# A narrow cross attention with its PSUM banks dealt anew and one small operation moved from VectorE to GpSimd

## The reference

```python
def _L0_xattn_ref(hidden_states, encoder_hidden_states, attention_mask, Wq, bq, Wk, bk, Wv, bv, Wo, bo):
    q = (hidden_states @ Wq.T + bq).reshape(B, N, H, D).transpose(0, 2, 1, 3)
    k = (encoder_hidden_states @ Wk.T + bk).reshape(B, T, H, D).transpose(0, 2, 1, 3)
    v = (encoder_hidden_states @ Wv.T + bv).reshape(B, T, H, D).transpose(0, 2, 1, 3)
    scores = jnp.einsum('bhnd,bhtd->bhnt', q, k) * scale + attention_mask[:, None, :, :]
    attn = jax.nn.softmax(scores, axis=-1)
    out = jnp.einsum('bhnt,bhtd->bhnd', attn, v)
    return out.transpose(0, 2, 1, 3).reshape(B, N, C) @ Wo.T + bo

x = x + _L0_xattn_ref(_layernorm(x, axis=-1), ctx_1024, mask_BxSxS2_ff0, ...)
```

## Time and profile before

| | |
|---|---|
| median of three executions | 2395.47 us |
| the profiled execution | 2399.14 us, span 2397.3 us |
| TensorE busy in the span | 2110.9 us (88%) |
| VectorE busy | 1924.7 us (80%) |
| ScalarE busy | 1668.8 us (70%) |
| GpSimd busy | 1200.5 us (50%) |
| narrow cross attention, first load's issue to last residual | 542.7 to 905.2 us |

### The profile page before, as it was taken

The page is one execution under the profiler, slowest core; times in us unless marked ns, Lnnn a source line. Parts: engine busy times, 40 slices in busy tenths (PEclk is TensorE's granted clock), DMA queues, the critical chain, the costliest instruction groups (busy, mean ns, idle before and its releaser), DMA issues. The chain is left out here.

```text
span 2397.3 us, 89507 instructions
## 1 busy us (share of the span) xinstructions
PE 2110.9 (88%) x32271; PEld 1771.4 (74%) x32271; DVE 1924.7 (80%) x5225; ACT 1668.8 (70%) x4485; POOL 1200.5 (50%) x1151
## 2 busy tenths in 40 slices
PE   7999999997777771537999979999799999999997
PEld 7888888885555550235888858888688888888886
DVE  3888888877999986996777667776498999999995
ACT  1676666666777775646888858888476776777674
POOL 0333333326777764107999869999132333333332
PEclk9999999998999995857999989999899999999998
DMA  5000000001111100001000000000133333333333
GB/s 125 3 0 0 0 0 0 0 1 32 31 30 30 30 25 1 1 0 37 1 0 0 0 2 1 0 0 0 52 110 105 115 117 111 115 109 118 113 112 91
DMA packets 112239, 96.98 MB, mean 40 GB/s; under 512 B 24259, under 2 KB 103430, under 8 KB 112134
## 3 DMA queue, kind: packets, MB, share of 16 engines
q1 hardware_dynamic: 108722, 94.39, 12.8%
q10 hardware_dynamic: 3412, 1.19, 0.2%
HBM read 53.59 MB, written 41.94 MB: 40 GB/s over the span
## 5 line engine op out<-in xcount | busy, mean ns | idle before, releaser
L706 POOL TENSOR_TENSOR sa_sc<-sa_sc,sa_rs 128x1024 f32<-128x1024 f32 x64 | 121.8, 1904 | 311.1 <-DVE sa_rs L682 311.1
L1870 POOL TENSOR_TENSOR lo_qk_r<-lo_qk_ms,w_neg_half 128x20 f32<-128x20 f32 x64 | 226.9, 3546 | 22.3 <-DVE lo_qk_ms L1792 22.3
L1870 POOL TENSOR_TENSOR gl_qk_r<-gl_qk_ms,w_neg_half 128x20 f32<-128x20 f32 x64 | 226.3, 3536 | 14.3 <-DVE gl_qk_ms L1792 14.0
L486 POOL TENSOR_TENSOR xan_ve<-xan_mv,w_eps_ln 128x1 f32<-128x1 f32 x64 | 12.1, 189 | 352.8 <-DVE xan_mv L480 352.8
L917 ACT ACTIVATE xa_vx<-xa_oo 64x512 f32<-64x512 f32 x256 | 151.3, 591 | 43.1 <-PE xa_oo L817 38.3
L1015 POOL TENSOR_TENSOR xa_sc<-xa_sc,xa_rs 128x1024 f32<-128x1024 f32 x64 | 122.2, 1909 | 107.3 <-DVE xa_rs L975 107.3
L930 ACT ACTIVATE xa_oT<-xa_oo 128x512 f32<-128x512 f32 x128 | 69.5, 595 | 131.4 <-PE xa_oo L864 131.4
L651 ACT ACTIVATE sa_oT<-sa_oo 128x512 f32<-128x512 f32 x128 | 69.5, 595 | 117.6 <-PE sa_oo L594 117.6
L827 PEld LDWEIGHTS xa_qs<-xan_xT,late_x_wq 128*128 128x128 f32 x1024 | 124.4, 192 | 30.6 <-issue 30.6
L909 ACT ACTIVATE xa_qT<-xa_qs,late_x_bq 128x128 f32<-128x128 f32 x512 | 138.9, 383 | 1.6
L558 PE MATMUL sa_qs<-san_xT,w_a_wq 128*128 128x128 f32 x1024 | 134.0, 285 | 5.4 <-DVE sa_sc L668 5.0
(11 more groups left out here) (323 smaller groups left out, 6714.0 us busy)
## 6 DMA issues: line engine op xcount, KB each, us to landing
blocks<-xa_tb SPq DMA_DIRECT2D x64, 512.0 KB, 2.7
xa_pt<-blocks SPq DMA_DIRECT2D x256, 128.0 KB, 2.9
w_x<-in_x_dram SPq DMA_DIRECT2D x8, 512.0 KB, 7.5
ca_cx<-in_ctx_dram SPq DMA_DIRECT2D x64, 64.0 KB, 1.8
ctxT_kept<-ca_xcT SPq DMA_DIRECT2D x64, 64.0 KB, 1.6
xa_cT<-ctxT_kept SPq DMA_DIRECT2D x64, 64.0 KB, 1.8
out_dram<-xa_out SPq DMA_DIRECT2D x64, 64.0 KB, 1.6
ca_mask<-in_mask_BxSxS_ff_dram SPq DMA_DIRECT2D x64, 32.0 KB, 1.7
```

The costliest lines, as they stand in the source:

```text
L706: pool.tensor_tensor(v, v, bcast(rs[:, s, :], 2, S), ALU.mult).then_inc(prob_done, 1)
L1870: pool.tensor_tensor(qk_r[:, s, :], qk_ms[:, s, :], k["neg_half"][:, 0:NQK], ALU.pow).then_inc(sg["qk_r"], 1)
```

## The change

Numerator and denominator get a bank of their own (`nd`), and the two waits quoted above go. In exchange the transposed probabilities have one bank (`pp`) in place of two: `turn_probs` and `probsT` become two pieces each of half the work, and the second four transposes wait for the copy of the first four. The offset of the norm goes from VectorE (one instruction) to GpSimd (two products of one column: minus the mean, and that times the power), together with a column of -1 set at the start. All lists but GpSimd's get another order, `output` goes from lag 7 to 6 and `residual` from 8 to 7. The sync queue's list is not edited.

```diff
-        off = sb("off", [P, 2])
+        off, neg_mean, neg_one = sb("off", [P, 2]), sb("neg_mean", [P, 2]), sb("neg_one", [P, 1])
         m1, m2 = ps("m1"), ps("m2")
-        pp = [ps("pp0"), ps("pp1")]
+        pp, nd = ps("pp"), ps("nd")
         ss = ctx.enter_context(nc.psum_tensor("ca_ss", [P, 4, 512], F32))
-        num, den = ss[:, 0, 256:384], ss[:, 0, 384:512]
+        num, den = nd[:, 0:P], nd[:, P:2 * P]
...
-                    after(pe, x_done, t, 7)
+                    after(pe, x_done, t, 6)
...
-                    after(pe, o_done, t, 4)
...
-                    pe.wait_ge(biased, min(t + 4, NT) * 2 if isinstance(t, int) else (t + 4) * 2)
...
-                def turn_probs(t, four):
-                    after(pe, exp_done, t)
-                    for b in range(2):
-                        after(pe, p_done, t, 1, per=2)
+                def turn_probs(b):
+                    def piece(t, four):
+                        after(pe, exp_done, t)
+                        if b == 0:
+                            after(pe, p_done, t, 1, per=2)
+                        else:
+                            pe.wait_ge(p_done, t * 2 + 1)
                         for n in range(4):
                             h = 8 * b + 2 * n
-                            last = pe.transpose(pp[b][:, n * P:(n + 1) * P],
-                                                sc[:, four, h:h + 2, :].rearrange("p a b -> p (a b)"), ident)
+                            last = pe.transpose(pp[:, n * P:(n + 1) * P], sc[:, four, h:h + 2, :].rearrange("p a b -> p (a b)"), ident)
                         last.then_inc(p_psum, 1)
+                    return piece
...
-                    pe.wait_ge(xT_done, min(t + 7, NT) if isinstance(t, int) else t + 7)
+                    pe.wait_ge(xT_done, min(t + 6, NT) if isinstance(t, int) else t + 6)
...
-                skewed(pe, NT, [(3, scores), (2, project), (1, turn), (6, attend), (5, turn_probs), (7, output)], 4)
+                skewed(pe, NT, [(6, attend), (3, scores), (5, turn_probs(0)), (2, project), (1, turn), (5, turn_probs(1)), (6, output)], 4)
...
-                skewed(act, NT, [(2, queries_keys), (1, turned), (2, values), (4, exponent), (5, probsT), (0, apply)], 4)
+                skewed(act, NT, [(5, probsT(0)), (2, queries_keys), (1, turned), (5, probsT(1)), (2, values), (4, exponent), (0, apply)], 4)
...
-                skewed(dve, NT, [(8, residual), (0, measure), (3, softmax), (6, normalise), (0, offset)], 4)
+                skewed(dve, NT, [(7, residual), (0, measure), (6, normalise), (3, softmax)], 4)
...
                 def rsqrt(t, four):
-                    norm_rsqrt(k, norm, pool, t, four % 2)
+                    s = four % 2
+                    after(pool, norm["mv_done"], t)
+                    pool.tensor_tensor(neg_mean[:, s:s + 1], norm["mv"][:, s, 0:1], neg_one[:, :], ALU.mult).then_inc(nm_done, 1)
+                    norm_rsqrt(k, norm, pool, t, s)
+                    after(pool, norm["rstd_done"], t)
+                    pool.tensor_tensor(off[:, s:s + 1], neg_mean[:, s:s + 1], norm["rstd"][:, s:s + 1], ALU.mult).then_inc(off_done, 1)
...
+                pool.memset(neg_one[:, :], -1.0).then_inc(minus, 1)
+                pool.wait_ge(minus, 1)
```

More of the change, by code:

```diff
@@ L1061, in narrow_cross_attention @@
                                                               sem("outT_psum"), sem("inverse"), sem("outT"))
-        y_psum, xb_done, x_done, off_done = sem("y_psum"), sem("x_plus_bias"), sem("x"), sem("offset")
+        y_psum, xb_done, x_done, off_done, nm_done, minus = sem("y_psum"), sem("x_plus_bias"), sem("x"), sem("offset"), sem("neg_mean"), sem("minus_one")
         with nc.Block() as block:
@@ L1183, in exponent, with probsT, piece @@
                     act.activation(sc[:, four, :, :], sc[:, four, :, :], ACT.Exp).then_inc(exp_done, 1)
[L1185 to L1188, removed]
+                def probsT(b):
+                    def piece(t, four):
+                        s = four % 2
+                        after(act, a_psum, t, 2)
                         act.wait_ge(p_psum, t * 2 + b + 1)
-                        act.activation(pt[:, s, 4 * b:4 * b + 4, :].rearrange("p a b -> p (a b)"), pp[b][:, :], ACT.Copy).then_inc(p_done, 1)
+                        act.activation(pt[:, s, 4 * b:4 * b + 4, :].rearrange("p a b -> p (a b)"), pp[:, :], ACT.Copy).then_inc(p_done, 1)
+                    return piece
                 def apply(t, four):
@@ L1206, in measure @@
                     norm_measure(k, norm, dve, tile_of(X, t), t, four % 2)
[L1208 to L1213, removed]
                 def softmax(t, four):
```

## The result

The median of four executions is **2356.71 us** (2352.11 to 2357.93); the kernel before, on the same chip, took 2395.30. The ratio is 0.9836, with a 95% interval of 0.9817 to 0.9856: 38.6 us or 1.6% faster. The forecast of 2363.5 was 6.8 us too slow; the time lies in its range, and close to what rival (1) gave.

What follows compares the result with a forecast made beforehand. A VectorE-GpSimd ring through shift and offset sets 5.43 us a step; the new longest ring is 4.89. 57 x (5.43 - 4.89) = 30.8, plus 1: 31.8 off 2399.1, less 3.7 to the runs' median: 2363.5 us, range 2352 to 2385.

Steps and rivals of the forecast that it cites:

- rival (1): ScalarE-TensorE handovers at their low ends, so VectorE's 4.78 us sets the step; 2357 us, chance 0.18.
- Offset to GpSimd: Moving the norm's offset takes one VectorE instruction a step, cuts the old ring, and adds two GpSimd products of 0.15 us.
- the ring above: Old step's ring across GpSimd and VectorE: shift, offset, residual, measure, bias, maximum, shift; 5.43 us a step.
- Own bank: Numerator and denominator's bank: scores and attend lose two waits at no instruction cost, letting attend go first and division precede bias.
- One bank for the transposes: ScalarE and TensorE alternate transposes and copies, exponent to exponent: 4.41 us plus four handovers of 0.12, a ring of 4.89.
- VectorE's floor: VectorE's remaining work per step: 1.20 us for reciprocal and product, 3.58 from residual to maximum, together 4.78.
- GpSimd: GpSimd's own step with the two new products at 0.15 us each: a floor of 4.56 us.
- sign against: VectorE's residual waiting for GpSimd's copy by more than 0.2 us would show the forecast wrong.
- rivals (3) and (4): ScalarE-TensorE handovers of 0.25 make the ring 5.41, about 2394 us, chance 0.05; of 0.34, 5.77, 2414 us, chance 0.09.
- Rival (2): Sync queue's context load lands late, at 3.0 us, making the step 5.24 us; 2383.5 us, chance 0.13.
- The sum: Narrow cross attention: 57 x (5.43 - 4.89) = 30.8 us, plus 1 at the end: 31.8 us saved.
- The end: From last shift to stage end, 11.3 us: 1 us saved by output and residual coming sooner, between nothing and 3.

Runs made afterwards that it cites:

- e1: Kernel before with only the norm's offset moved from VectorE to GpSimd; 2392.77 us, ratio 0.9971.
- e2: Kernel before with the offset left on VectorE, but reading one tensor and the power as a column of scalars; 2390.25 us, ratio 0.9957.
- e6: Changed kernel with the offset back on VectorE in its old form, last in its list, without GpSimd's two products; 2357.39 us, ratio 0.9827.
- e5: Changed kernel with GpSimd's residual copy one tile earlier and ScalarE's values behind the exponent; 2345.38 us, ratio 0.9782.
- e3: Changed kernel with only GpSimd's residual copy one tile earlier (lag 5); 2358.06 us, ratio 0.9823.
- e12: Changed kernel with numerator and denominator back in the scores' bank, VectorE dividing first, scores behind the second transposes; 2464.00 us, ratio 1.0278.
- e10: Changed kernel with eight steps instead of four in the body of each compute engine's loop; 2355.33 us, ratio 0.9840.
- e11: e5 with eight steps instead of four in the body of each compute engine's loop; 2346.92 us, ratio 0.9801.

## Why the prediction was right, and where it was not

*Offset to GpSimd* is the step that failed: "VectorE loses one instruction a step and the ring above is cut", and the 0.54 us a step were booked on that. Cut alone, that ring gives 0.09 (e1, e2), and in the new order the wait is gone without the move (e6). Of the mechanism one half was right, that the offset waits for the shift. The Trainium skill's page "SBUF — State Buffer", section "SBUF: two separate sides", says the same of a VectorE operation with two inputs in SBUF: it is shut out for as long as a GpSimd operation that reads SBUF and began before it runs. The rows agree: 754 ns with two tensors, 203 with one. That the time came right in spite of this step is in part luck: the sum sets the measured old step against the longest ring of the new kernel and never asks which part of the change gives the difference. The same reasoning, used for e1, gave 2361 to 2372 us, and 2392.77 were measured.

*Own bank*: "Both go at no cost in instructions; they allow attend to be first", and nothing was booked for it. Together with the order it carries the whole gain (e6). The sentence that hid it is "TensorE, ScalarE and the loads have room in it". The idle time was there, but two of the waits in the earlier trace rows, the values' 0.74 for the attend and the turn's 0.86 for the normed rows, were links of a second ring of 5.51. Busy time could not show it; following those two waits one step on would have.

*One bank for the transposes*: that a ring of ScalarE and TensorE from exponent to exponent sets the new step was right; its size was off, and so was its middle. The ring is 4.70 and not 4.89: its four gaps, taken as 0.12 each, are 0.05, 0.04, 0.08 and 0.14, together 0.31 for 0.48, and the last is no handover. The sentence that didn't hold is "Project and turn (TensorE) and keys, queries and turned context (ScalarE) lie inside it beside the copies": projections, keys, queries and turned context end 0.10 later than the way through the second transposes. The loop's head adds 0.06 to 0.07 a step, which no term held. In these rows the second four's wait for the first copy therefore lengthens nothing. The 0.11 us a step that the prediction had the alternation cost has no run beside it, since none turns the probabilities through two banks in the new order.

*VectorE's floor* was read as 4.78 and is at most 4.48. The rows were taken from start to end with the gaps in them for the work's own length: from the measure's second instruction to the next operation 0.32 passed there (729.10 to 729.42) and 0.10 pass now (721.85 to 721.95). Rival (1), whose 2357 the time met, is therefore not what happened: VectorE waits for the copy in the changed kernel, and e5's step of 4.61 lies below that "floor".

*GpSimd*: its own step is 4.45, a little under the forecast 4.56, and the two products came as forecast (0.14 each, forecast 0.15). The residual's wait for the copy, named as a sign against, is there with 0.26, and costs nothing (e3). Handovers of 0.34 in the ring, rivals (3) and (4), weren't seen. Rival (2) isn't in the changed kernel, whose turn hardly waits for the load (0.3 us in all), but it is what holds e12.

*The sum*: the gain between first and last shift is 337.3 - 302.0 = 35.3 us, from the earlier trace rows and their two rows in the changed kernel:

```profile
L1251 POOL TENSOR_TENSOR ca_sc<-ca_sc,ca_mx x64: 1899/1902/1910, 556.8 to 858.8; 128x1024 f32<-128x1024 f32 x64
```

```profile
869.52 0.29 DVE L1235 TENSOR_TENSOR w_x<-ca_m,ca_xb 128x128 f32<-128x128 f32 x1 [0.58 <-PE ca_m L1151]
```

57 x (5.43 - 4.76) would be 38.2; the first intervals are up to 0.6 longer than the steady ones and take the 2.9 back. The end gave 0.3, not 1 (last shift 858.8, last residual's end 869.81: 11.0 us, 11.3 before), and the first shift comes 0.3 later behind the first load (14.2 us, 13.9 before). Forecast 31.8, measured 35.3 in the stage; the other 3.3 of the medians' 38.6 belong to no part of the change that I can name, and are less than the rest of the kernel differs from execution to execution.

## What to carry to other kernels

Before a stall is booked as gain, look for other rings of the same length: start from every wait that repeats each step, and follow it through the order of the in-order queues as well as through the data. An engine that is idle a fifth of each step can still be a link of a ring. A bank or a buffer may be worth no more than the order that it allows; here the two weren't told apart. To find out, change the order with and without it, one edit at a time.

## What the runs showed of the hardware that was not expected

- A product of one column on VectorE took 0.75 us at the median beside GpSimd's shift with two tensors as inputs, and 0.20, never over 0.216, with one tensor and a column of scalars.
- Handovers between ScalarE and TensorE took 0.04 to 0.08 us where the receiving engine was waiting already; the 0.34 of the earlier trace rows is not the price of one.
- A pass through the loop's head costs the step that it stands in 0.22 to 0.28 us in the changed kernel and in e10, and 0.43 in e11.
